# Window attention and convolution on one core: heads in two groups of 64 rows, separate stacks for the transposed pass, maxima sent between partitions

## The chip, the core and the metric
The kernel runs on one core of a Trainium2 chip. The metric is device time in microseconds (us) of one execution; 1663.28 us is the median of three runs before the change.

## The reference, cut to what matters
The input is 2 images of 128 channels, 128 x 128 pixels. Two layers, each with a group normalisation (32 groups) ahead of it and a residual sum behind:
```
x = x + attention(_gn(x))     # L0
x = x + conv3x3(_gn(x))       # L1

g = clip((x*ac_w + ac_b)*x, 0, 6);  qkv = einsum(g, qkv_w)      # 3 x 128 channels
q, k, v: windows of 8x8 pixels (64 tokens), 16 heads of 8 channels
attn = softmax(q @ k.T * 8**-0.5) ; o = attn @ v                # 64 x 64 per window and head
out = einsum(o, proj_w) + proj_b
```
There are 512 windows, and a 64 x 64 score matrix for each of them and each head.

## The kernel before
The kernel goes through each image in 32 units of 8 windows (512 tokens). A unit passes seven stages named by letters, which overlap: `G` (the clipped product, led by 4 iterations), `H` (its f16 high and low halves, 3), `B` (Q, K and V products for unit n + 2), `C` (scores and row maxima for unit n + 1), `D` (first half of the transposed pass for unit n), `E` (its second half, for n - 1), `R` (residual and statistics, n - 2). `iterations` (L189) peels the first and last iterations and runs the middle in a loop whose turn holds `BUFS` = 3 units. Each engine has its own program in a fixed order written by hand in `one`; `after(engine, semaphore, unit)` (L171) is the wait for a step of a unit. After the 32 units of an image come 16 units of the convolution (`conv_one`).

A head has only 8 channels. Q and K are therefore kept in f16 with high and low halves, three parts of 8 rows each (24 rows a head), and four heads share a stack of 96 partitions. TensorE computes the product (`project`, L850), ScalarE copies its high half (L475 for Q, L485 for K), VectorE takes the low half (L681, L688), and SP writes both to a scratch in DRAM (`write`, L261: two DMAs) and reads them back in the stacked order: Q in one DMA (L286), K in four (L290), one for each place of a head in the block diagonal of `k_stack`. TensorE's `scores` (L866) then has 8 matmuls for a pair of windows: 64 tokens of Q times the block-diagonal K of four heads, 256 columns. VectorE takes row maxima (`row_max`, L668). When the four pairs of a unit are through, TensorE transposes the maxima (L976), ScalarE and VectorE make two halves of them (L469, L675), and SP writes them to DRAM (L274) and reads them into rows 96 to 103 of `q_stack` (L277). There they meet the constant rows of `k_stack` (-4096, set by L444 with `mask4`), so that the transposed scores come with the maximum subtracted. `scores_t` (L878) has 32 matmuls of 64 columns a pair, over all 128 rows; ScalarE takes the exponential of 1024 columns (`exps`, L457); `weigh` (L891) multiplies by V in fp32 with 16 matmuls of 18 columns, which the trace shows as 32. Outputs are divided (L657, L660), turned (`turn`, L913), copied in two halves (`turned`, L464) and projected (`output`, L920).

SP has one program and issues all DMAs in its order; a wait on it holds all that stands behind it. In PSUM, bank `GA` (6) takes Q's product and the turned output, bank `GB` (7) K's and V's products and the projected output.

## Time and profile before

| | us |
|---|---|
| median of 3 runs | 1663.28 |
| lowest, highest | 1657.38, 1670.82 |
| the profiled execution | 1678.25 |
| its span | 1676.5 |
| mean granted TensorE clock | 0.828 of full |

The span is the time between the first and the last instruction of the profiled execution. The attention of the first image lies between about 60 and 680 us of it, that of the second between about 890 and 1490 us; the convolutions follow each. A block of matmuls in the timeline shows the time from the start of its first to the end of its last, the tail of the last one in the array included. PEld is the weight load, which overlaps PE. PEclk is the granted clock as a share of 2.4 GHz, 0.50 being 1.2 GHz.

### The profile page before, as it was taken

The numbers are of one execution on the slowest core, as the hardware profiler recorded it, in microseconds if no ns is written. First come the engines' busy times: TensorE is split into PE (matmuls) and PEld (weight loads), VectorE is DVE, ScalarE is ACT, GpSimd is POOL, SyncE is SP. The second block draws the span as 40 slices with busy tenths as digits, with TensorE's granted clock in tenths as the row PEclk, the third lists the DMA queues.
The fourth block names the chain that finished last, engine by engine and source line by source line (L and its number), as shares of the span: only waits on it lengthen the run. The fifth ranks groups of instructions, "written<-read, shape, count | busy, mean of one in ns | idle before, by whom it ended". The sixth has DMA issues, their size and how long they took to land. (4 is left out here: it accounts for less than half of the span.)

```text
span 1676.5 us, 57125 instructions
## 1 busy us (share of the span) xinstructions
PE 1296.1 (77%) x23523; PEld 854.3 (51%) x23523; DVE 1005.9 (60%) x1379; ACT 782.4 (47%) x1107; POOL 380.2 (23%) x245
## 2 busy tenths in 40 slices
PE   1388787887878888597874888888889888859876
PEld 0166565555655666433322656656656666643332
DVE  7555445454544454399994555455654565439998
ACT  3545444444544453344432545454544465435443
POOL 5001111111111110255551111111111111025665
PEclk9778768887887797599995888788985799859998
DMA  5223222232322231012232322332322233200111
GB/s 221 76 91 108 79 75 92 81 90 82 108 83 82 81 115 48 1 55 96 100 130 98 117 85 92 93 95 83 118 83 80 89 113 98 66 2 38 50 50 63
DMA packets 113491, 142.86 MB, mean 85 GB/s; under 512 B 19440, under 2 KB 89584, under 8 KB 112240
## 3 DMA queue, kind: packets, MB, share of 16 engines
q1 hardware_dynamic: 113264, 139.31, 26.1%
q8 instruction: 206, 3.38, 0.8%
q14 instruction: 21, 0.17, 0.0%
HBM read 70.06 MB, written 69.21 MB: 83 GB/s over the span
## 5 line engine op out<-in xcount | busy, mean ns | idle before, releaser
L457 ACT ACTIVATE work<-ps,ws 128x1024 f32<-128x1024 f32 x256 | 285.0, 1113 | 490.4 <-PE ps L886 485.9
L668 DVE TENSOR_REDUCE m_all<-ps 128x16 f32<-128x1024 f32 x256 | 311.9, 1219 | 181.1 <-PE ps L873 179.2
L904 PEld LDWEIGHTS ps<-v_ext,work 128*64 128x64 f32 x8192 | 320.2, 158 | 81.6 <-ACT work L457 64.8
L904 PE MATMUL ps<-v_ext,work 128*64 128x18 f32 x8192 | 328.7, 225 | 39.4 <-ACT work L457 30.2
L873 PE MATMUL ps<-k_stack,q_stack 96*64 96x256 f16 x2048 | 190.3, 315 | 162.7 <-DMA k_stack<-stack_scratch 93.7
L372 POOL TENSOR_TENSOR g_lo<-work,g_hi 128x512 f16<-128x512 f32 x64 | 74.2, 1159 | 1003.0 <-ACT g_hi L493 1003.0
L873 PEld LDWEIGHTS ps<-k_stack,q_stack 96*64 96x64 f16 x2048 | 107.5, 123 | 269.1 <-issue 252.9
L886 PEld LDWEIGHTS ps<-q_stack,k_stack 128*64 128x64 f16 x8192 | 178.4, 124 | 75.6 <-issue 75.3
L886 PE MATMUL ps<-q_stack,k_stack 128*64 128x64 f16 x8192 | 205.2, 209 | 4.6 <-issue 4.2
L836 PE MATMUL ps<-work,c_hi 128*128 128x512 f16 x384 | 152.2, 396 | 68.4 <-DVE work L756 68.3
L681 DVE TENSOR_TENSOR work<-ps,work 128x512 f16<-128x512 f32 x64 | 44.3, 692 | 242.3 <-ACT work L475 242.3
L543 ACT CAST work<-work 128x640 f16<-128x640 f32 x128 | 91.9, 719 | 147.9 <-DVE work L752 106.4
L756 DVE TENSOR_TENSOR work<-work 128x640 f16<-128x640 f32 x128 | 152.3, 1193 | 5.4 <-ACT work L543 5.1
L837 PE MATMUL ps<-work,c_lo 128*128 128x512 f16 x384 | 151.4, 394 | 0.0
L838 PE MATMUL ps<-work,c_hi 128*128 128x512 f16 x384 | 151.0, 393 | 0.0
L398 POOL TENSOR_TENSOR work<-work 128x640 f32<-128x640 f32 x64 | 113.9, 1782 | 49.1 <-DVE work L756 21.5
L920 PE MATMUL ps<-work,pw 128*128 128x512 f32 x128 | 113.3, 981 | 0.9 <-ACT work L464 0.9
L377 POOL TENSOR_TENSOR img<-img,work 128x512 f32 (+1 forms) x64 | 81.3, 1270 | 126.0 <-ACT work L479 126.0
L836 PEld LDWEIGHTS ps<-work,c_hi 128*128 128x128 f16 x384 | 38.5, 100 | 139.6 <-DVE work L756 81.7
L386 POOL TENSOR_TENSOR work<-work,img 128x1024 f32<-128x1024 f32 x30 | 84.6, 2819 | 102.8 <-DVE work L736 102.8
L752 DVE TENSOR_TENSOR work<-work 128x640 f32<-128x640 f32 x64 | 91.8, 1437 | 4.7 <-issue 2.4
L736 DVE SCALAR_TENSOR_TENSOR work<-ps,ws,work 128x512 f32<-128x512 f32 x128 | 92.3, 742 | 0.5 <-ACT work L527 0.2
(125 smaller groups left out, 1660.3 us busy)
## 6 DMA issues: line engine op xcount, KB each, us to landing
stack_scratch<-work SPq DMA_DIRECT2D x128, 256.0 KB, 2.1
q_stack<-stack_scratch SPq DMA_DIRECT2D x64, 384.0 KB, 3.9
k_stack<-stack_scratch SPq DMA_DIRECT2D x256, 96.0 KB
stack_scratch<-work SPq DMA_DIRECT2D x128, 128.0 KB, 2.1
out_dram<-work SPq DMA_DIRECT2D x32, 512.0 KB, 2.7
img<-in_x_dram SPq DMA_DIRECT2D x8, 1024.0 KB, 14.2
img<-in_x_dram SPq DMA_DIRECT2D x16, 512.0 KB, 3.8
max_scratch<-m_pair SPq DMA_DIRECT2D x64, 32.0 KB, 1.8
```

Source lines behind the costliest of these rows:

```text
L398: g.tensor_tensor(plane[2 * k + 1], column(cx, 1), column(cx, c), op).then_inc(odd_planes, 1)
L457: a.activation(probs[:, p % 2, :], ps[:, ST_B:ST_B + 2, :].rearrange("p w t -> p (w t)"), ACT.Exp, scale=ws[:, R_EXP:R_EXP + 1]).then_inc( ...
L668: v.tensor_reduce(m_all[:, 0, :, p, :], ps[:, S_B:S_B + 2, :].rearrange("p h (g j k) -> p (h g) j k", g=2, k=WIN), AX.X, ALU.max).then_inc ...
L736: v.scalar_tensor_tensor(out=outputs(c_out[par], to), in0=ps[:, PLANES * par + m, :], scalar=ws[:, col:col + 1], in1=outputs(c_out[par], old),
L756: v.tensor_tensor(x_lo[:, i, :, :], plane[i], x_hi[:, i, :, :], ALU.subtract).then_inc(x_lo_done, 1)
L836: t_.matmul(o, lhs_hi, rhs_hi, start=first, stop=False)
L837: t_.matmul(o, lhs_lo, rhs_hi, start=False, stop=False)
L838: return t_.matmul(o, lhs_hi, rhs_lo, start=False, stop=last)
L873: mm = t_.matmul(ps[64 * w:64 * w + 64, S_B + h, gg * 256:gg * 256 + 256], q_stack[0:ROWS, mc, 2 * h + gg, tok], k_stack[0:ROWS, mc, 2 * h ...
L886: mm = t_.matmul(ps[64 * e:64 * e + 64, ST_B + w, hp * WIN:(hp + 1) * WIN], k_stack[:, md, g, j + e, tok], q_stack[:, md, g, tok], start=T ...
L904: mm = t_.matmul(ps[64 * w:64 * w + 64, PV_B + p // 2, col:col + VC], probs[:, p % 2, at:at + WIN], v_ext[:, md, 2 * p + w, hp, :], start= ...
L920: t_.matmul(ps[:, GB, :], pw[:, :], o_t, start=True, stop=True).then_inc(proj_done, 1)
```

## The change
The 16 heads are kept in two groups of 64 partitions (`HR` = 2), and each group in four stacks (`HG` = 4) of two heads (`HJ` = 2): 48 rows. A score matmul takes 48 rows, 64 stationary columns and 128 moving columns, and writes one half of the PSUM partitions; row group r writes bank `S_B + r`. So it uses a quarter of the array, and `scores` has 16 of them a pair. The transposed pass no longer uses the same stacks: `scores_t` takes plain K (`k_pl`) as the stationary side and block-diagonal Q (`q_bd`) as the moving side, 50 rows with the two rows of maxima, 128 columns, 16 matmuls a pair. So Q and K are both read from DRAM twice, once for each pass, in the stage before each; each stack has two buffers in place of three. The maxima's halves go in four DMAs from 32 partitions of `m_pair` each straight to one row of `q_bd`. The loop's turn holds 6 units. K's product moves to the head of the iteration, V's product moves to bank `GA` behind Q's, the output takes `GB` after K. ScalarE copies the turned output at once. Constants are set by memsets alone; the projection's input channels are permuted as the weights are loaded, in two DMAs.

```diff
--- before.py
+++ after.py
...
-HG, HJ = 4, 4
+HR, HG, HJ = 2, 4, 2
 PAIRS = UW // 2
 PARTS = 3
 ROWS = HJ * HD * PARTS
-MROWS = 2 * HJ
+HROWS = HD * PARTS
 HP = HEADS // 2
 VC = 2 * HD + 2
 BUFS = 3
+TWO = 2
+TURN = 6
...
-        q_stack = sb("q_stack", [P, BUFS, HG, UT], F16)
-
-
-        k_stack = sb("k_stack", [P, BUFS, HG, HJ, UT], F16)
+        q_pl = sb("q_pl", [P, TWO, HG, UT], F16)
+        k_bd = sb("k_bd", [P, TWO, HG, HJ, UT], F16)
+
+        k_pl = sb("k_pl", [P, TWO, HG, UT], F16)
+        q_bd = sb("q_bd", [P, TWO, HG, HJ, UT], F16)
...
-        m_all = sb("m_all", [P, 2, HG, PAIRS, HJ])
+        m_all = sb("m_all", [P, 2, HEADS, PAIRS])
...
-            first, turns = 2, (UNITS - 6) // BUFS
+            first, turns = 2, (UNITS - 6) // TURN
             for i in range(-4, first):
                 if i == -2 and late:
                     late()
-                one(i, i % BUFS, active(i))
+                one(i, i % TURN, active(i))
+            for i in range(first + turns * TURN, UNITS + 2):
+                one(i, i % TURN, active(i))
...
-            return ps[rows, GB, :].rearrange("p (a d) -> p a d", d=HD)
+            return ps[rows, GA, :].rearrange("p (a d) -> p a d", d=HD)
...
-            sp.wait_ge(pool_set, 12)
-            sp.wait_ge(act_step, 9)
+            sp.wait_ge(pool_set, 10)
 
             for b in range(BATCH):
                 def one(i, m, on):
                     n = i + b * UNITS
-                    n_r = HD * PARTS
-
-                    def write(d, mb, which):
-                        lo, hi, into, sent = ((q_lo_done, q_hi_done, q_in, q_sent),
-                                              (k_lo_done, k_hi_done, k_in, k_sent))[which]
-                        after(sp, into, d - 1)
+                    def write(d, which):
+                        lo, hi, sent = ((q_lo_done, q_hi_done, q_sent), (k_lo_done, k_hi_done, k_sent))[which]
                         after(sp, lo, d)
                         after(sp, hi, d)
-                        to = stackd[mb, which]
+                        to = stackd[(m + 2) % BUFS, which]
                         sp.dma_start(to[:, 0:2, :], qk[:, 2 * which:2 * which + 2, :]).then_inc(sent, 16)
                         sp.dma_start(to[:, 2, :], qk[:, 1 + which, :]).then_inc(sent, 16)
+
+                    def plain(to, src, event):
+                        rows = src.rearrange("(r g a) s t -> r (a s) g t", r=HR, g=HG)
+                        for r in range(HR):
+                            sp.dma_start(to[64 * r:64 * r + ROWS, :, :], rows[r]).then_inc(event, 16)
+
+                    def spread(to, src, event):
+                        rows = src.rearrange("(r g j d) s t -> r j (d s) g t", r=HR, g=HG, j=HJ)
+                        for r in range(HR):
+                            for j in range(HJ):
+                                at = 64 * r + HROWS * j
+                                sp.dma_start(to[at:at + HROWS, :, j, :], rows[r, j]).then_inc(event, 16)
                     if "D" in on:
-                        after(sp, m_in, n - 1)
                         after(sp, m_hi_done, n)
                         after(sp, m_lo_done, n)
-                        sp.dma_start(maxd[m], m_pair[:, :, :]).then_inc(m_sent, 16)
-                        after(sp, m_sent, n)
-                        after(sp, st_done, n - BUFS)
-                        sp.dma_start(q_stack[ROWS:ROWS + MROWS, m, :, :].rearrange("r g (p t) -> r (g p) t", p=PAIRS),
-                                     maxd[m].rearrange("(a j) s t -> (j s) a t", j=HJ)).then_inc(m_in, 16)
+                        after(sp, st_done, n - TWO)
+                        for r in range(HR):
+                            for k in range(2):
+                                at = 64 * r + ROWS + k
+                                sp.dma_start(q_bd[at:at + 1, m % TWO, :, :, :].rearrange("o g j (p t) -> o (g j p) t", p=PAIRS),
+                                             m_pair[32 * r:32 * r + 32, k, :]).then_inc(m_in, 16)
                     if "B" in on:
-                        d, mb = n + 2, (m + 2) % BUFS
-                        k_rows = stackd[mb, 1].rearrange("(g j d) s t -> j (d s) g t", g=HG, j=HJ)
-                        write(d, mb, 0)
-                        write(d, mb, 1)
-                        after(sp, q_sent, d)
-                        after(sp, st_done, d - BUFS)
-                        sp.dma_start(q_stack[0:ROWS, mb, :, :],
-                                     stackd[mb, 0].rearrange("(g r) s t -> (r s) g t", g=HG)).then_inc(q_in, 16)
-                        after(sp, k_sent, d)
-                        for j in range(HJ):
-                            sp.dma_start(k_stack[n_r * j:n_r * j + n_r, mb, :, j, :], k_rows[j]).then_inc(k_in, 16)
+                        after(sp, qd_in, n)
+                        after(sp, kd_in, n)
+                        write(n + 2, 1)
+                        write(n + 2, 0)
+                        after(sp, kc_in, n + 1)
+                        after(sp, qc_in, n + 1)
+                        after(sp, k_sent, n + 2)
+                        after(sp, s_done, n)
+                        spread(k_bd[:, m % TWO, :, :, :], stackd[(m + 2) % BUFS, 1], kc_in)
+                        after(sp, q_sent, n + 2)
+                        plain(q_pl[:, m % TWO, :, :], stackd[(m + 2) % BUFS, 0], qc_in)
+                    if "C" in on:
+                        if "B" not in on:
+                            after(sp, qd_in, n)
+                            after(sp, kd_in, n)
+                        after(sp, st_done, n + 1 - TWO)
+                        spread(q_bd[:, (m + 1) % TWO, :, :, :], stackd[(m + 1) % BUFS, 0], qd_in)
+                        plain(k_pl[:, (m + 1) % TWO, :, :], stackd[(m + 1) % BUFS, 1], kd_in)
...
-                    def turned(d, h):
-
-                        after(act, ot_done, d, h + 1)
+                    def turned(d):
+
+                        after(act, ot_done, d)
                         after(act, proj_done, d - 1)
-                        a.copy(o_t[:, 256 * h:256 * h + 256], ps[:, GA, 256 * h:256 * h + 256]).then_inc(ot_out, 1)
+                        a.copy(o_t, ps[:, GA, :]).then_inc(ot_out, 1)
 
                     if "D" in on:
                         after(act, mt_done, n)
-                        after(act, m_sent, n - 1)
+                        after(act, m_in, n - 1)
                         a.mul(m_pair[:, 0, :], ps[0:PAIRS * HEADS, M_B, 0:P], 1.0 / PAIR_MAX).then_inc(m_hi_done, 1)
+                    if "B" in on:
+                        after(act, k_done, n + 2)
+                        after(act, k_sent, n + 1)
+                        a.copy(qk[:, 2, :], ps[:, GB, :]).then_inc(k_hi_done, 1)
...
-                        v.tensor_reduce(m_all[:, 0, :, p, :],
-                                        ps[:, S_B:S_B + 2, :].rearrange("p h (g j k) -> p (h g) j k", g=2, k=WIN), AX.X,
+                        v.tensor_reduce(m_all[:, 0, :, p],
+                                        ps[:, S_B:S_B + 2, :].rearrange("p r (a k) -> p (r a) k", k=WIN), AX.X,
                                         ALU.max).then_inc(max_done, 1)
                     if peeled(i, 0) and b:
                         after(dve, out_done, b * CUNITS - 1)
@@ -677,16 +680,15 @@
                     if "C" in on:
                         row_max(0)
                     if "B" in on:
+                        after(dve, k_hi_done, n + 2)
+                        v.tensor_tensor(qk[:, 3, :], ps[:, GB, :], qk[:, 2, :], ALU.subtract).then_inc(k_lo_done, 1)
...
-                        for h in range(2):
-                            for gg in range(2):
-                                for w in range(2):
-                                    tok = slice((2 * p + w) * WIN, (2 * p + w + 1) * WIN)
-                                    mm = t_.matmul(ps[64 * w:64 * w + 64, S_B + h, gg * 256:gg * 256 + 256],
-                                                   q_stack[0:ROWS, mc, 2 * h + gg, tok],
-                                                   k_stack[0:ROWS, mc, 2 * h + gg, :, tok], start=True, stop=True)
+                        settle(pe)
+                        for g in range(HG):
+                            for w in range(2):
+                                tok = slice((2 * p + w) * WIN, (2 * p + w + 1) * WIN)
+                                for r in range(HR):
+                                    rows = slice(64 * r, 64 * r + ROWS)
+                                    mm = t_.matmul(ps[64 * w:64 * w + 64, S_B + r, g * P:g * P + P],
+                                                   q_pl[rows, (m + 1) % TWO, g, tok], k_bd[rows, (m + 1) % TWO, g, :, tok],
+                                                   start=True, stop=True)
                         mm.then_inc(s_done, 1)
 
                     def scores_t(d, md, p):
 
                         after(pe, exp_done, d, p)
+                        settle(pe)
                         for w in range(2):
                             tok = slice((2 * p + w) * WIN, (2 * p + w + 1) * WIN)
-                            for hp in range(HP):
-                                g, j = hp // 2, 2 * (hp % 2)
-                                for e in range(2):
-                                    mm = t_.matmul(ps[64 * e:64 * e + 64, ST_B + w, hp * WIN:(hp + 1) * WIN],
-                                                   k_stack[:, md, g, j + e, tok], q_stack[:, md, g, tok],
+                            for g in range(HG):
+                                h, c = g // 2, g % 2
+                                for r in range(HR):
+                                    rows = slice(64 * r, 64 * r + ROWS + 2)
+                                    at = w * 256 + h * P
+                                    mm = t_.matmul(ps[64 * c:64 * c + 64, ST_B + r, at:at + P],
+                                                   k_pl[rows, md % TWO, g, tok], q_bd[rows, md % TWO, g, :, tok],
...
+                        project(1, GB, k_done)
                     if "C" in on:
-                        after(pe, q_in, n + 1)
-                        after(pe, k_in, n + 1)
+                        after(pe, qc_in, n + 1)
+                        after(pe, kc_in, n + 1)
                         scores(0)
                     if "E" in on:
                         weigh(n - 1, me, 1)
+                        scores_t(n - 1, me, 2)
                     if "B" in on:
-                        after(pe, g_lo_done, n + 2)
-                        after(pe, q_lo_done, n + 1)
+                        after(pe, v_out, n + 1)
                         after(pe, ot_out, n - 2)
-                        if peeled(i, -2) and b:
-                            after(pe, m3_out, b * CUNITS - 1)
                         project(0, GA, q_done)
-                    if "E" in on:
-                        scores_t(n - 1, me, 2)
-                    if "R" in on:
-                        if "C" in on:
-                            after(pe, v_out, n + 1)
-                        output(n - 2)
                     if "C" in on:
                         scores(1)
                     if "E" in on:
                         weigh(n - 1, me, 2)
-                    if "B" in on:
-                        after(pe, v_out, n + 1)
-                        after(pe, res_done, n - 2)
-                        project(1, GB, k_done)
+                    if "R" in on:
+                        if "B" in on:
+                            after(pe, k_lo_done, n + 2)
+                        after(pe, res_done, n - 3)
+                        output(n - 2)
                     if "E" in on:
                         scores_t(n - 1, me, 3)
-                        if "B" in on:
-                            after(pe, q_lo_done, n + 2)
-                        after(pe, ot_out, n - 2)
-                        turn(n - 1, 0)
+                    if "B" in on:
+                        after(pe, q_lo_done, n + 2)
+                        v_rows()
                     if "C" in on:
                         scores(2)
                     if "E" in on:
                         weigh(n - 1, me, 3)
                     if "D" in on:
                         after(pe, m_in, n)
+                        after(pe, qd_in, n)
+                        after(pe, kd_in, n)
                         scores_t(n, m, 0)
-                    if "B" in on:
-                        after(pe, k_lo_done, n + 2)
-                        v_rows()
+                    if "E" in on:
+                        if "B" in on:
+                            after(pe, v_out, n + 2)
+                        after(pe, ot_out, n - 2)
+                        turn(n - 1, 0)
...
```

SP's program, one unit in the peeled iterations behind the loop, before (`max_scratch` and `stack_scratch` are DRAM, `m_pair` holds the maxima, `work` the halves of Q and K):
```order
L274 DMA max_scratch<-m_pair 64x256
L277 DMA q_stack<-max_scratch 8x16x128
L268 DMA stack_scratch<-work 128x1024
L269 DMA stack_scratch<-work 128x512
L268 DMA stack_scratch<-work 128x1024
L269 DMA stack_scratch<-work 128x512
L286 DMA q_stack<-stack_scratch 96x4x512
L290 DMA k_stack<-stack_scratch 24x4x512 x4
```
and now:
```order
L288 DMA q_bd<-m_pair 1x32x128 x4
L267 DMA stack_scratch<-work 128x1024
L268 DMA stack_scratch<-work 128x512
L267 DMA stack_scratch<-work 128x1024
L268 DMA stack_scratch<-work 128x512
L280 DMA k_bd<-stack_scratch 24x4x512 x4
L273 DMA q_pl<-stack_scratch 48x4x512 x2
L280 DMA q_bd<-stack_scratch 24x4x512 x4
L273 DMA k_pl<-stack_scratch 48x4x512 x2
```
The eleven issues of a unit are twenty. K's write comes first, K's read for the scores stands behind both writes, and the second reading (`q_bd`, `k_pl`) is of the unit one ahead of its use.

TensorE's program in the loop, from the transpose of the maxima on, before (`k_stack,q_stack` are scores at L873, `q_stack,k_stack` transposed scores, L904 weighted sums, L836 to L838 first Q's product, then K's):
```order
L976 MATMUL ps<-ident,m_all 128x128
L873 MATMUL ps<-k_stack,q_stack 64x256 x8
L904 MATMUL ps<-v_ext,work 64x18 x16
L836 MATMUL ps<-g_hi,w_hi 128x512
L837 MATMUL ps<-g_hi,w_lo 128x512
L838 MATMUL ps<-g_lo,w_hi 128x512
L886 MATMUL ps<-q_stack,k_stack 64x64 x32
L920 MATMUL ps<-work,pw 128x512
L873 MATMUL ps<-k_stack,q_stack 64x256 x8
L904 MATMUL ps<-v_ext,work 64x18 x16
L836 MATMUL ps<-g_hi,w_hi 128x512
L837 MATMUL ps<-g_hi,w_lo 128x512
```
and now (L876 scores, L892 transposed scores, L910 weighted sums, L838 to L840 first K's product, then Q's):
```order
L986 MATMUL ps<-ident,m_all 128x128
L838 MATMUL ps<-g_hi,w_hi 128x512
L839 MATMUL ps<-g_hi,w_lo 128x512
L840 MATMUL ps<-g_lo,w_hi 128x512
L876 MATMUL ps<-k_bd,q_pl 64x128 x16
L910 MATMUL ps<-v_ext,work 64x18 x16
L892 MATMUL ps<-q_bd,k_pl 64x128 x16
L838 MATMUL ps<-g_hi,w_hi 128x512
L839 MATMUL ps<-g_hi,w_lo 128x512
L840 MATMUL ps<-g_lo,w_hi 128x512
L876 MATMUL ps<-k_bd,q_pl 64x128 x16
L910 MATMUL ps<-v_ext,work 64x18 x16
```
K's product has come ahead of the first scores, and Q's stands behind the first transposed block.

## Rows read from the trace of the kernel before

**Rows 1.** The page's engine totals: busy us (share of the span) xinstructions
```profile
PE 1296.1 (77%) x23523; PEld 854.3 (51%) x23523; DVE 1005.9 (60%) x1379; ACT 782.4 (47%) x1107; POOL 380.2 (23%) x245
```

**Rows 2.** Timeline of SP's queue, first and last issue of the maxima in each batch (columns: start us, us, engine line op out<-in xcount)
```profile
82.21 0.52 SPq L274 DMA_DIRECT2D max_scratch<-m_pair  x1
...
645.26 0.45 SPq L274 DMA_DIRECT2D max_scratch<-m_pair  x1
...
914.62 0.49 SPq L274 DMA_DIRECT2D max_scratch<-m_pair  x1
...
1464.76 0.45 SPq L274 DMA_DIRECT2D max_scratch<-m_pair  x1
```

**Rows 3.** Timeline of all engines, 302 to 320 us: one passage of K through DRAM
```profile
302.05 0.68 DVE L688 TENSOR_TENSOR work<-ps,work 128x512 f16<-128x512 f32 x1
...
303.27 0.93 SPq L269 DMA_DIRECT2D stack_scratch<-work  x1
...
305.68 1.56 SPq L290 DMA_DIRECT2D k_stack<-stack_scratch  x4
...
310.60 0.63 PE L873 MATMUL ps<-k_stack,q_stack 96*64 96x256 f16 x8 [1.86 <-DMA k_stack<-stack_scratch]
...
318.26 0.58 ACT L485 CAST work<-ps 128x512 f16<-128x512 f32 x1 [1.28 <-PE ps L838]
...
318.87 0.69 DVE L688 TENSOR_TENSOR work<-ps,work 128x512 f16<-128x512 f32 x1
```

**Rows 4.** Waits of all engines (us in total, times, longest us), and two timeline rows of PE
```profile
PE ps L873 <- DMA k_stack<-stack_scratch: 93.7, 45, 3.7
...
PE ps L873 <- issue: 67.9, 18, 6.3
...
402.69 0.33 PE L976 MATMUL ps<-ident,m_all 128*128 128x128 f32 x1 [0.25 <-DVE m_all L668]
406.87 1.06 PE L873 MATMUL ps<-k_stack,q_stack 96*64 96x256 f16 x8 [3.85 <-issue]
```

**Rows 5.** Windows: us, busy of PE, PEld, DVE, ACT, POOL, then PEclk, DMA share, GB/s
```profile
310.00:311.00 1.00, 0.40 (x8) 0.41 (x10) 0.00 (x0) 0.00 (x0) 0.00 (x0) 1.00 0.00 0
312.00:313.00 1.00, 1.00 (x8) 0.44 (x7) 0.49 (x1) 0.00 (x0) 0.00 (x0) 0.50 0.14 35
980.00:1460.00 480.00, 408.11 (x9300) 298.26 (x9302) 252.45 (x367) 241.61 (x366) 62.23 (x52) 0.83 0.31 92
```

**Rows 6.** Timeline, 300 to 303.2 us: TensorE's blocks with the clock at 1.00
```profile
300.41 0.39 PE L836 MATMUL ps<-g_hi,w_hi 128*128 128x512 f16 x1
...
300.85 0.38 PE L838 MATMUL ps<-g_lo,w_hi 128*128 128x512 f16 x1
...
301.16 0.70 PE L886 MATMUL ps<-q_stack,k_stack 128*64 128x64 f16 x32
...
301.78 0.44 PE L913 MATMUL ps<-ident,work 128*128 128x128 f32 x2
...
302.19 0.63 PE L873 MATMUL ps<-k_stack,q_stack 96*64 96x256 f16 x8
...
303.14 1.11 PE L904 MATMUL ps<-v_ext,work 128*64 128x18 f32 x32 [0.32 <-ACT work L457]
```

**Rows 7.** The page's costliest groups (columns as on the page: busy, mean ns | idle before)
```profile
L457 ACT ACTIVATE work<-ps,ws 128x1024 f32<-128x1024 f32 x256 | 285.0, 1113 | 490.4 <-PE ps L886 485.9
L668 DVE TENSOR_REDUCE m_all<-ps 128x16 f32<-128x1024 f32 x256 | 311.9, 1219 | 181.1 <-PE ps L873 179.2
```

**Rows 8.** The page's DMA issues: KB each, median us from issue to landing
```profile
q_stack<-stack_scratch SPq DMA_DIRECT2D x64, 384.0 KB, 3.9
k_stack<-stack_scratch SPq DMA_DIRECT2D x256, 96.0 KB
stack_scratch<-work SPq DMA_DIRECT2D x128, 128.0 KB, 2.1
```

117 lines of the change are left out of this document (51 added, 66 removed).

## The prediction
> **What bounds the kernel now.** The profiled execution took 1678.25 us (span 1676.5), 0.9% over the median of the three timed runs, 1663.28. The engine totals come first: TensorE is the busiest, 77% of the span [rows 1]. To see where the time lies I took the issue of the maxima (L274), once per unit, as a beat: 31 periods from 82.21 to 645.26 us and 31 from 914.62 to 1464.76 us [rows 2], together 1113.2 us for 62 periods, **17.95 us per unit**. The other 563 us (start, convolutions, pipeline ends) the change hardly touches.
>
> In the timeline one unit shows a ring [rows 3]. K's low half leaves VectorE at 302.05 + 0.68; its write is issued until 304.2; the four reads that wait for it start at 305.68; TensorE, idle for 1.86 us, starts the next unit's scores at 310.60 when they have landed. The same queue of TensorE has that iteration's K product only shortly before 318.26, where ScalarE, idle for 1.28 us, copies it; K's low half comes at 318.87. From one low half to the next it is 16.8 us: 0.7 for itself, 7.9 of write and read, 7.7 inside TensorE's queue from scores to K product, 0.6 of copy. So **the ring through DRAM** ends last in many units, with TensorE's own work close behind.
>
> Two rows tell of what the ring costs besides. TensorE stood before the first scores for 93.7 us on DMAs, and for 67.9 us in 18 stops without a releaser, the longest 6.3 us, a typical one 3.85 us at 406.87 us [rows 4]. Two of the 18 belong to the fillings of the two batches; 16 are as many as the loop of three units has turns (2 x 8). I read those, (67.9 - 2 x 6.3) / 16 = 3.5 us each, as the price of a back jump, which here lies over the wait for DMAs. And the granted clock is 1.00 before such a gap, 0.50 at 312 us after TensorE has resumed (the 1.2 GHz level), and over 480 us of the second batch 0.83 [rows 5]: a third of the time at half speed.
>
> **The change part by part**, per unit, at the 2.4 GHz level.
> *Scores and transposed scores.* Eight 256-column matmuls take 0.63 us, of which about 0.2 is the tail of the last one; 32 of 64 columns take 0.70 us and hold the engine 0.50 us, 16 ns each [rows 6]. So column halves already run side by side (64 columns at 2.4 GHz are 27 ns). Afterwards both kinds are 16 matmuls of 128 columns on quarters of the array. Bounds for a block: all four quarters together 16 x 53 / 4 = 0.21 us; only column halves together 0.43 us; one after another 0.85 us. No row shows 64-row matmuls. I take 0.25 us (16 times the 16 ns pace [rows 6]), nearest in form. Saved: 4 x (0.45 - 0.25) + 4 x (0.50 - 0.25) = 1.8 us.
> *Changes of array shape.* From L838 to L886 the distance is 0.31 us against (300.85 - 300.41) / 2 = 0.22 us between products, so a switch costs 0.09 us; L886 to L913 is 0.62 us against 0.50 us, again 0.1 [rows 6]. Before, 10 switches per unit; afterwards 17, since weighted sums (full rows) and scores (half rows) alternate. +0.7 us. The upper bound is a whole tail of 0.2 us at each of the 17: 3.4 in place of 1.0, so +2.4 us, and the block gain would be gone; I take the rows' own 0.1. The Trainium skill (TensorEngine Tiling (Array Packing), Key Properties) says that a change of tiling mode, not of tile alone, drains TensorE. By that rule, the trace agrees in kind and puts it at half a tail; a full drain is in rival 3.
> *TensorE's sum.* At the fast level, a unit before is scores 1.8, transposed scores 2.0, weighted sums 4 x 0.9, two products 1.3, V 0.8, output 1.0, transposes 1.2, switches 1.0: about 12.7 us ([rows 6]; V is 48 times 16 ns, the output four times a product's 0.22 us and a little more). After: 12.7 - 1.8 + 0.7 = **11.6 us**.
> *The order.* K's product goes to the head of the iteration, V behind Q. The ring is now the one of Q. Walk, t = 0 at the first scores: row maximum until 1.7 (1.22 each [rows 7]), K's low half until 2.4, its write at once; weighted sums until 1.2, transposed block, exponentials until 3.0 (1.11 each [rows 7]), Q copy until 3.6, low half until 4.3, write issued until 5.2 (Q's product ends at 2.5). Then the four K reads are issued (4 x 0.39 [rows 3]), Q's write has landed (2.1 us after issue [rows 8]) at 7.0, two Q reads until 7.8, and 3.4 us after the last issue (as 307.2 to 310.6 [rows 3]) all has landed: the ring is **11.2 us** instead of 16.8.
> *Rest of the walk.* TensorE: second weighted sums from 3.0, output 4.0 to 4.9, transposed block, V until 6.1, scores, weighted sums at 7.1 (exponentials end 7.0, held by the residual's evacuation), transposed block 8.3; ScalarE then evacuates V and g and ends the next exponentials at 9.9; weighted sums until 10.9, transposed block, transposes, K product at 12.9. TensorE idles 0.6 + 0.8 us in it. So **13.0 us** with all at full clock; ScalarE and VectorE were busy 241.61 and 252.45 us in some 27 units [rows 5], 8.9 and 9.4 us each: neither binds.
> *DMA queue.* 11 issues per unit become 20 (4 one-row sends of maxima, 4 writes, 12 reads): 20 x 0.39 = 7.8 us of SP. The second reading of the stacks (6 issues, 2.3 us) comes after Q's reads, at 7.8 to 10.2, lands by 13.6 to 15, and the next K write waits for it at 13.0 + 2.4 = 15.4: hidden, by less than 2 us. If that cover is gone, it is added to the ring. Bytes: 1.6 MB become 2.34 MB (two more stacks of 384 KB [rows 8]). At 92 GB/s for a share of 0.31 [rows 5] a MB costs 3.4 us of all engines: 7.9 us of a unit, 60%.
> *Maxima.* They go straight to one partition, without the round through DRAM. That round is not on the ring (issued at the unit's end, wanted in its second half): zero either way. Merged o_t copy: 0.15 us of ScalarE, covered by TensorE. The new waits of the output on K's low half and of V on Q's are met at 2.4 and 4.3, before 4.0 and 5.3: zero.
> *Clock.* Gaps of 0.6 and 0.8 us stand in place of one of 2 to 4 us; the products behind 300.41 us have lengths of the full level (0.38 us) with gaps of 0.3 us about them [rows 6]. I leave 0.6 us per unit: 13.6 us.
> *Back jumps.* Six units per turn: 2 x 4 = 8 in place of 16, but now uncovered: 3.5 us each and some 2.5 us lost to half speed behind it (5 us at 0.50) = 48 us. Bounds: 4 us each (32 us) to 8 us each (64 us).
> *Start.* Memsets and mask rows change, and the projection weights arrive in 32-byte pieces; bounds -4 to +6 us, as ScalarE's and VectorE's start-up work overlaps the image load. Zero.
>
> **Sum.** 62 x 13.6 = 843, plus 48 = 891 in place of 1113: -222 us. 1678 - 222 = 1456 us for a profiled execution; the shown median lies 15 us under its own, so **1441 us**. Its own range: 12.8 per unit with 32 us of jumps (-287) to 14.4 with 64 (-156): 1376 to 1507.
>
> **Rivals.**
> 1. *The ring stays in the lead.* 60% of DMA share with the second reading in the way of K's write: ring and second reading in line cost 4.5 us more than 11.2, so 15.7 per unit, with the jumps hidden in it again: 62 x 15.7 = 973, -140: 1523 us. For it: the slack is under 2 us. Against: K's and Q's reads are ahead of the second reading in the queue.
> 2. *The clock keeps falling.* With 0.83 as before, 13.0 / 0.83 = 15.7 us, jumps 8 x 3.5 = 28 us: 62 x 15.7 + 28 = 1001, -112: 1551 us. For it: the gaps at 310 and 403 us were followed by half speed [rows 4, 5]. Against: no such gap is left outside jumps.
> 3. *No packing over row halves.* 0.43 us per block: 8 x 0.18 = 1.4 us more, x 62 = +89: 1530 us. With switches at a whole tail besides, 1.7 us more, +105: 1635 us, hardly a change. The page named above, read at its strictest, speaks for that far end.
> 4. *Slower.* Quarter blocks run one after another, their weight loads and shape changes between them. The decisive point: with jumps spread over the units the forecast is 14.4 us, so the period is back at 17.95 when a block holds TensorE for (17.95 - 14.4) / 8 + 0.25 = 0.69 us. At 0.85 us (16 x 53 ns in a row) it is 14.4 + 4.8 = 19.2 us: 62 x 19.2 = 1190, +77: 1740 us. For it: no row shows this form. Against: 32 narrow loads and matmuls passed in 0.50 us [rows 6], 16 ns where a single file would take 27.
> 5. *It doesn't shorten anything*, since a wait I don't see (a late residual, second buffers of two in place of three) holds the period: 1650 to 1670.
>
> **Chances.** Forecast 0.60; rival 1 0.12; rival 2 0.08; rival 3 0.08 (a quarter of it near no change); rival 4 0.07; rival 5 0.05; together 1.00. A measurement of this kernel tells 1% from no change. Faster 0.60 + 0.12 + 0.08 + 0.06 = 0.86, within 1% 0.02 + 0.05 = 0.07, slower 0.07. The range takes the forecast's own and rivals 1 to 3 but for their far ends: **1375 to 1580**.
>
> **What will show it.** In the changed trace: the beat of the maxima near 13.6 us; new score blocks starting 16 ns apart and lasting about 0.45 us with the tail; the first scores waiting for no DMA outside jumps; K's low half 2.4 us behind the first scores; a granted clock above 0.93 in the attention stages; 8 stops of about 3.5 us before the K product, now the first instruction of a turn. A block over 0.69 us would make rival 4 true; scores waiting for q_pl, or K's write waiting for q_bd, rival 1; a clock still at 0.83 with no DMA wait, rival 2.

## The result: slower, with TensorE at half clock

The changed kernel takes **1818.29 us** (median of four runs, 1816.38 to 1822.06); the kernel before took 1664.78 beside it. The ratio is **1.093**, 95% interval 1.088 to 1.098. The forecast was 1441 us, in a range of 1375 to 1580: wrong in size and in sign. The profiled execution took 1822.06 us, span 1820.3, at a mean granted clock of 0.670; the other three had 0.640 to 0.642. Below, one of the two runs each of experiments nine and eleven fell in a slower state of the chip (1670.86 and 1720.25 us), so their times are those of the other run.

The page of the changed kernel, the lines that answer to [rows 1, 7, 8] (columns as on that page; the PEclk line holds the granted clock in tenths, 40 slices):
```profile
PE 1474.0 (81%) x21475; PEld 930.1 (51%) x21475; DVE 991.4 (54%) x1379; ACT 772.1 (42%) x1039; POOL 376.5 (21%) x243
...
PEclk9996656555555655599975555565555565558999
...
q1 hardware_dynamic: 168960, 187.58, 38.8%
...
L671 DVE TENSOR_REDUCE m_all<-ps 128x16 f32<-128x1024 f32 x256 | 312.2, 1220 | 371.8 <-PE ps L876 371.8
L910 PE MATMUL ps<-v_ext,work 128*64 128x18 f32 x8192 | 446.9, 262 | 60.2 <-ACT work L462 60.1
L462 ACT ACTIVATE work<-ps,ws 128x1024 f32<-128x1024 f32 x256 | 284.4, 1111 | 303.7 <-PE ps L892 302.2
...
L876 PE MATMUL ps<-k_bd,q_pl 48*64 48x128 f16 x4096 | 151.3, 289 | 18.4 <-DMA q_pl<-stack_scratch 11.1
...
q_pl<-stack_scratch SPq DMA_DIRECT2D x128, 192.0 KB, 3.7
```
VectorE and ScalarE work as long as before (1220 and 1111 ns) and wait longer, both for TensorE's score blocks. The wait of the scores for DMAs is nearly gone: 11.1 us against 93.7 [rows 4]. The PEclk line shows nines only at its ends and between the two batches; the attention stages read mostly 5 and 6 tenths. The nines up to 142 us are an error of the record, since the blocks there have the lengths that they have at 0.50:
```profile
105.00:120.00 15.00, 14.74 (x221) 9.96 (x223) 6.83 (x10) 6.21 (x10) 0.30 (x1) 1.00 0.36 94
...
110.34 1.90 PE L910 MATMUL ps<-v_ext,work 128*64 128x18 f32 x32
```
So this execution's 0.670 is too high, and the 0.64 of the other three is nearer.

Windows of the changed kernel (columns as in [rows 5]), the attention stages and two short stretches:
```profile
80.00:720.00 640.00, 560.98 (x9599) 384.94 (x9599) 285.23 (x417) 280.70 (x385) 69.12 (x58) 0.61 0.46 116
980.00:1600.00 620.00, 544.21 (x9452) 371.89 (x9447) 280.18 (x413) 276.94 (x381) 68.66 (x58) 0.58 0.48 119
390.00:421.00 31.00, 29.30 (x444) 19.43 (x446) 14.16 (x21) 11.82 (x17) 2.38 (x2) 0.50 0.41 106
423.00:426.00 3.00, 1.91 (x66) 1.51 (x54) 1.91 (x3) 1.60 (x3) 0.00 (x0) 1.00 0.95 218
```
TensorE is busy 88% of the stages, more than before (408.11 of 480, 85%), and the clock is 0.61 and 0.58 (the first is 0.56 from 160 us on, without the stretch of the error) where it was 0.83 [rows 5]. From 390 to 421 us it is busy 29.30 of 31 us and stands at 0.50, the 1.2 GHz level, throughout. No stop of TensorE explains that: the 1.7 us in which it idles are spread over the stretch.

Its timeline, the same blocks at both levels (405 to 409 us at 0.50, 423 to 425 us at 1.00), and the maxima in SP's queue, which answer to [rows 2]:
```profile
405.78 0.64 PE L876 MATMUL ps<-k_bd,q_pl 48*64 48x128 f16 x16
406.87 1.90 PE L910 MATMUL ps<-v_ext,work 128*64 128x18 f32 x32 [0.45 <-ACT work L462]
408.70 0.64 PE L892 MATMUL ps<-q_bd,k_pl 50*64 50x128 f16 x16
...
422.79 0.42 PE L876 MATMUL ps<-k_bd,q_pl 48*64 48x128 f16 x16
423.13 1.11 PE L910 MATMUL ps<-v_ext,work 128*64 128x18 f32 x32
424.18 0.42 PE L892 MATMUL ps<-q_bd,k_pl 50*64 50x128 f16 x16
```
```profile
76.17 1.26 SPq L288 DMA_DIRECT2D q_bd<-m_pair  x2
...
411.75 2.41 SPq L288 DMA_DIRECT2D q_bd<-m_pair  x4
432.26 3.11 SPq L288 DMA_DIRECT2D q_bd<-m_pair  x4
...
721.28 1.14 SPq L288 DMA_DIRECT2D q_bd<-m_pair  x2
...
972.07 1.16 SPq L288 DMA_DIRECT2D q_bd<-m_pair  x2
...
1605.34 1.14 SPq L288 DMA_DIRECT2D q_bd<-m_pair  x2
```
The beat is (721.28 - 76.17 + 1605.34 - 972.07) / 62 = **20.62 us** instead of 17.95, which is 1278.4 us in place of 1113.2 for the 62 periods: +165.2 us. All else became 21 us shorter (the beat's first row comes 6 us earlier, the way between the batches is 18.6 us shorter, the end 3 us longer). The sum, +144, is the measured difference of the two profiled executions. At the full level the block fits the prediction: from 422.79 to the weighted sums' start it is 0.34 us, where 0.25 and a switch of 0.1 were forecast (the rows show only their sum). It is hardly ever at that level.

The waits of the changed kernel (engine, line waited for: us, times, longest):
```profile
DVE m_all L671 <- PE ps L876: 371.8, 138, 6.2
ACT work L462 <- PE ps L892: 302.2, 134, 5.5
...
DVE st L698 <- POOL img L387: 212.4, 56, 5.1
...
PE ps L838 <- issue: 20.5, 6, 3.8
```
The third line is a second surprise: VectorE stands 212.4 us, in 56 of 64 units, before the statistics of the image (L698) for GpSimd's residual addition. The kernel before has the same wait in as many places, but shorter:
```profile
DVE st L696 <- POOL img L377: 78.3, 56, 4.9
```
The last line of the changed kernel's waits has the stops at the back jumps, six and not eight: a loop of four turns jumps back three times, in two batches.

### The profile page after: what moved, and what is told of

It reads as the page before. It is cut to its first block and busy times, and to the rows that moved or that the text cites. A ratio compares the mean times of both kernels' runs of the same rounds, so it can differ in the third digit from the quotient of the medians.

```text
span 1820.3 us, 53510 instructions
## 1 busy us (share of the span) xinstructions
PE 1474.0 (81%) x21475; PEld 930.1 (51%) x21475; DVE 991.4 (54%) x1379; ACT 772.1 (42%) x1039; POOL 376.5 (21%) x243
## 5 line engine op out<-in xcount | busy, mean ns | idle before, releaser
L671 DVE TENSOR_REDUCE m_all<-ps 128x16 f32<-128x1024 f32 x256 | 312.2, 1220 | 371.8 <-PE ps L876 371.8
L910 PE MATMUL ps<-v_ext,work 128*64 128x18 f32 x8192 | 446.9, 262 | 60.2 <-ACT work L462 60.1
L910 PEld LDWEIGHTS ps<-v_ext,work 128*64 128x64 f32 x8192 | 419.1, 207 | 108.9 <-ACT work L462 72.2
L462 ACT ACTIVATE work<-ps,ws 128x1024 f32<-128x1024 f32 x256 | 284.4, 1111 | 303.7 <-PE ps L892 302.2
L838 PE MATMUL ps<-work,c_hi 128*128 128x512 f16 x384 | 151.2, 394 | 68.3 <-DVE work L758 68.2
L876 PE MATMUL ps<-k_bd,q_pl 48*64 48x128 f16 x4096 | 151.3, 289 | 18.4 <-DMA q_pl<-stack_scratch 11.1
L876 PEld LDWEIGHTS ps<-k_bd,q_pl 48*64 48x64 f16 x4096 | 94.5, 144 | 136.9 <-issue 133.5
L698 DVE BATCH_NORM_STATS2 st<-img (+1 forms) x64 | 44.4, 693 | 212.4 <-POOL img L387 212.4
L892 PE MATMUL ps<-q_bd,k_pl 50*64 50x128 f16 x4096 | 153.1, 292 | 0.0
L488 ACT ACTIVATE work<-ps,vecs,ws 128x512 f32<-128x512 f32 x64 | 49.7, 777 | 243.2 <-PE ps L926 243.2
L840 PE MATMUL ps<-work,c_hi 128*128 128x512 f16 x384 | 150.5, 392 | 0.0
L892 PEld LDWEIGHTS ps<-q_bd,k_pl 50*64 50x64 f16 x4096 | 95.4, 145 | 101.1 <-issue 93.6
L500 ACT COPY v_ext<-ps 64x512 f32<-64x512 f32 x128 | 75.9, 593 | 118.8 <-PE ps L910 103.3
L919 PE MATMUL ps<-ident,work 128*128 128x128 f32 x256 | 76.0, 392 | 61.5 <-ACT v_ext L500 60.9
L838 PE MATMUL ps<-g_hi,w_hi 128*128 128x512 f16 x128 | 79.1, 618 | 44.6 <-issue 20.5
L838 PEld LDWEIGHTS ps<-work,c_hi 128*128 128x128 f16 x384 | 38.3, 100 | 139.7 <-DVE work L758 82.1
```

The costliest lines, as they stand in the source:

```text
L462: a.activation(probs[:, p % 2, :], ps[:, ST_B:ST_B + 2, :].rearrange("p w t -> p (w t)"), ACT.Exp, scale=ws[:, R_EXP:R_EXP + 1]).then_inc( ...
L671: v.tensor_reduce(m_all[:, 0, :, p], ps[:, S_B:S_B + 2, :].rearrange("p r (a k) -> p (r a) k", k=WIN), AX.X, ALU.max).then_inc(max_done, 1)
L838: t_.matmul(o, lhs_hi, rhs_hi, start=first, stop=False)
L840: return t_.matmul(o, lhs_hi, rhs_lo, start=False, stop=last)
L876: mm = t_.matmul(ps[64 * w:64 * w + 64, S_B + r, g * P:g * P + P], q_pl[rows, (m + 1) % TWO, g, tok], k_bd[rows, (m + 1) % TWO, g, :, tok] ...
L892: mm = t_.matmul(ps[64 * c:64 * c + 64, ST_B + r, at:at + P], k_pl[rows, md % TWO, g, tok], q_bd[rows, md % TWO, g, :, tok], start=True, s ...
```

## The experiments

Two questions: what took the clock, and where the ring's gain went. As to the first, one theory is that the granted clock follows **how much of the array is at work**, and that the new forms (48 or 50 rows of a tile in place of 96 or 128, half the multiplies or less) took it. Its rivals are the new order, the added DMA traffic, and the added changes of array shape. A ratio is always to the kernel before, timed on the same chip (1676 to 1685 us there, against 1664.78 beside the changed kernel itself); a clock is the mean of the profiled execution (nine's is that of its one run), and between runs of one kernel it differs by up to 0.04. In four and thirteen the record errs at the start as it does in the changed kernel; their clocks are too high by 0.01 to 0.03, an estimate from the lengths of the weighted sums.

**One: double the work** of the changed kernel. Every quarter matmul of both kinds is issued twice, to the same place.
```diff
-                                    mm = t_.matmul(ps[64 * w:64 * w + 64, S_B + r, g * P:g * P + P],
-                                                   ...
+                                    for again in range(2):
+                                        mm = t_.matmul(ps[64 * w:64 * w + 64, S_B + r, g * P:g * P + P],
+                                                       ...
```


> The changed kernel with every quarter-array score matmul (scores and transposed scores) issued twice; the second overwrites the first with the same values. A block then streams 32 x 128 columns on quarters, as long as the kernel before streamed in a block (0.43 us at full clock, 0.85 at half). Theory A (the full clock is granted only where TensorE's time is filled with streaming columns; the change halved the streaming of the scores): the mean granted clock rises from 0.67 to over 0.80 and the time falls under 1818, to 1550 to 1700 us, although there is more work. Theory B (quarter-array matmuls don't count for the clock): clock 0.60 to 0.67, 8 x 0.43 us more a unit at half clock, 1990 to 2050 us. Theory C (the new order with its many short stops costs the clock, not the matmuls' form): as B.

Measured: 1756.05 us, ratio 1.040 (1.027 to 1.054), clock 0.742. Twice the matmuls in the blocks, and less time: 1756 against 1818 us, ratio 1.040 against 1.093. The gain is smaller than theory A asked (under 1700 us, a clock over 0.80), but no account in which TensorE's work or its switches bind at a fixed clock allows that.

**Two: the same matmuls on all 128 rows.** The other half's rows of the 16 matmuls meet data that don't belong to them, so the scores of the two groups of heads are added to each other. Here and in ten, thirteen and sixteen the rows of `q_pl` that hold no data are set to zero once, at the start.
```diff
-                                    rows = slice(64 * r, 64 * r + ROWS)
+                                    rows = slice(0, P)
...
-                                    rows = slice(64 * r, 64 * r + ROWS + 2)
+                                    rows = slice(0, P)
```


> The changed kernel with each score matmul over all 128 rows (both groups of heads at once) in place of 48 or 50; columns, counts, banks and order as in the changed kernel. The scores of the two groups are added to each other, so the output is not the reference's. A block streams 16 x 128 columns on halves of the array: 0.43 us at full clock, twice the quarter blocks. Theory A: like the doubled kernel, clock over 0.80, 1550 to 1700 us. Theory B: also over 0.80. Theory C: clock 0.60 to 0.67 and 1990 to 2050 us.

Measured: 1680.09 us, ratio 1.004 (1.000 to 1.008), clock 0.828. The number of matmuls and columns, the order and the DMAs are those of the changed kernel; the packing of row halves is lost; and it is 1680 us in place of 1818 (1.004 against 1.093). DMA traffic (133 GB/s at 80 to 600 us here) is excluded as what takes the clock.

**Three and five: the two parts of the change apart.** Three keeps the stacks, forms and maxima of before, and takes the new order on all engines with six units per turn. Five is the reverse: new forms, stacks, direct maxima and six per turn, in the old order.
```diff
+TURN = 6
...
-                        write(d, mb, 0)
                         write(d, mb, 1)
-                        after(sp, q_sent, d)
+                        write(d, mb, 0)
+                        after(sp, k_sent, d)
...
```


> The kernel before with the new order alone: K's product at the head, V behind Q, K's write first, the output behind K, the turned output copied at once, six units a turn; stacks, score matmuls (96 and 128 rows, half arrays) and the maxima's way through DRAM as before. Theories A and B: TensorE streams as much as before without the long wait for K's reads, so the mean granted clock is over 0.90, the period 14 to 15 us and the time 1470 to 1550 us. Theory C: clock under 0.70 and 1850 us or more.

> The changed kernel with the order of the kernel before on TensorE, ScalarE, VectorE and in SP's writes and reads (Q first, V in bank GB, the turned output in two copies): the quarter-array scores, separate stacks, direct maxima and six units a turn remain. Theory B2 (the clock goes by what the matmuls put on the array, and quarter blocks put less on it, in any order): granted clock 0.62 to 0.72 and 1780 to 1900 us, the slowness of the change is in the form. Theory C2 (form and new order together): clock over 0.78, 1640 to 1720 us.

Measured: three 1695.11 us, 1.010 (1.005 to 1.015), clock 0.819; five 1787.39 us, 1.061 (1.054 to 1.068), clock 0.657. So the **forms** bring the low clock and most of the loss in either order; the order does not. (Five has the stacks and the direct maxima too, but so has two, with a clock of 0.828.) But the order alone, which takes the ring away and takes 14 back jumps down to 6, brings nothing either: both theories A and B had expected a clock over 0.90 and 1470 to 1550 us of it. That is the second question, and the timeline of experiment three answers it, here 403 to 411 us:
```profile
403.06 0.68 PE L884 MATMUL ps<-q_stack,k_stack 128*64 128x64 f16 x32
...
403.32 1.21 ACT L496 COPY v_ext<-ps 64x512 f32<-64x512 f32 x2 [1.27 <-PE ps L902]
...
404.56 0.62 ACT L503 CAST g_hi<-work 128x512 f16<-128x512 f32 x1
...
405.25 1.15 POOL L373 TENSOR_TENSOR g_lo<-work,g_hi 128x512 f16<-128x512 f32 x1 [14.93 <-ACT g_hi L503]
...
406.37 1.26 POOL L378 TENSOR_TENSOR img<-img,work 128x512 f32 x1
...
407.96 0.69 DVE L694 BATCH_NORM_STATS2 st<-img  x1 [3.88 <-POOL img L378]
...
408.57 1.21 DVE L667 TENSOR_REDUCE m_all<-ps 128x16 f32<-128x1024 f32 x1
...
409.84 0.33 PE L975 MATMUL ps<-ident,m_all 128*128 128x128 f32 x1 [1.47 <-DVE m_all L667]
...
410.04 0.38 PE L834 MATMUL ps<-g_hi,w_hi 128*128 128x512 f16 x1
...
410.77 0.63 PE L871 MATMUL ps<-k_stack,q_stack 96*64 96x256 f16 x8
```
The idle times behind the rows lead through four engines' work in single file: the weighted sums let ScalarE copy V, then cast g; GpSimd forms g's low half (14.93 us idle, waiting for it), and only behind that, in program order, adds the residual; VectorE's statistics wait 3.88 us for it, and the last row maximum is queued behind them; its transpose, the K product and the next scores come last. This chain replaced the ring. The wait in it is VectorE's, 3.88 us here and 211.5 us in all, against 78.3 in the kernel before.

**Four and six: fill the array from outside.** One, then two, full-array matmuls of 512 columns ahead of each score block of the changed kernel, overwritten by it.
```diff
+                        for pad in range(1):
+                            t_.matmul(ps[:, S_B, :], w_hi[:, 0, :], c_hi[:, 0:4, :].rearrange("p a d -> p (a d)"), start=True, stop=True)
```


> The changed kernel with one full-array matmul of 512 columns on constant weights ahead of each score block (4 a unit); its result is overwritten by the scores. Pure extra work: 4 x 0.43 us a unit at half clock, 4 x 0.22 at full. Theory A: mean clock over 0.75, time 1500 to 1700 us. Theory B: the full-array columns count, so the same, if less. Theory C: clock 0.60 to 0.67, 62 x 1.7 us more, 1900 to 1950 us.

> The changed kernel with two full-array matmuls of 512 columns ahead of each score block (8 a unit): as much extra streaming as doubling (e1) or widening (e2) gave, 8 x 0.43 us at half clock, but on 128 rows and 128 columns and in one piece. Theory A (only streaming time counts): clock 0.74 to 0.83 as in e1 and e2, 1700 to 1800 us. Theory B2 (what counts is how full the array is over the stretches in which scores and weighted sums alternate; extra work in one place doesn't help the other stretches): clock 0.68 to 0.72, 1880 to 1930 us.

Measured: one 1864.44 us, 1.106 (1.095 to 1.116), clock 0.686; two 1771.33 us, 1.053 (1.047 to 1.060), clock 0.727. The first filler cost more than it gave, the second gave back more than both cost. Neither expectation for six (under 1800 us at a clock of 0.74 or more; 1880 us or more at 0.72 or less) fits both of its numbers, so this pair doesn't decide between them.

**Seven and eight: GpSimd's two steps exchanged,** the residual ahead of g's low half, in experiment three (seven) and in the changed kernel (eight).
```diff
-                    if "H" in on:
-                        after(pool, g_hi_done, n + 3)
-                        g.tensor_tensor(g_lo[:, m, :], g32, g_hi[:, m, :], ALU.subtract).then_inc(g_lo_done, 1)
                     if "R" in on:
...
+                    if "H" in on:
+                        after(pool, g_hi_done, n + 3)
+                        g.tensor_tensor(g_lo[:, m, :], g32, g_hi[:, m, :], ALU.subtract).then_inc(g_lo_done, 1)
```


> The kernel of e3 (old forms, new order) with two instructions of GpSimd exchanged: the residual sum goes ahead of g's low half. In e3 the chain weighted sums, V's copy, g's high half, g's low half, residual sum, statistics, last row maximum, transpose of the maxima (403.2 to 409.8 us) sets the period at full clock, not the DMA ring. If so, the last row maximum comes 1.5 to 2.5 us earlier, the period at full clock falls from 16 to 17 us to 14.5 to 15, the clock rises over 0.85 and the time falls to 1560 to 1620 us, under the kernel before. If the chain isn't the bound: 1680 to 1700 us.

> The changed kernel with the same exchange on GpSimd. VectorE no longer stands 3.9 us for the residual ahead of the last row maximum. If the half clock is the bound (TensorE busy 88% of the attention stages at a clock near 0.6), the gain is small: 1770 to 1815 us, clock 0.65 to 0.70. If the stops of TensorE are what lowers its clock, the clock rises over 0.75 and the time falls under 1700 us.

Measured: seven **1534.45 us**, 0.912 (0.906 to 0.919), clock 0.868; eight 1800.45 us, 1.072 (1.066 to 1.077), clock 0.633. On the old forms, behind the new order, the exchange is worth 0.098 of 1680, 164 us, more than the 75 to 135 us that were expected; on the new ones, where half-clock TensorE binds, about a fifth of that. The exchange in the old order was not tried. Waits and windows of seven:
```profile
POOL img L375 <- ACT work L484: 715.2, 64, 18.5
POOL g_lo L378 <- ACT g_hi L503: 276.9, 64, 33.9
```
```profile
80.00:600.00 520.00, 446.05 (x11028) 333.91 (x11028) 294.84 (x434) 287.97 (x400) 72.64 (x60) 0.88 0.32 99
850.00:1300.00 450.00, 394.07 (x9503) 295.24 (x9504) 258.14 (x379) 253.14 (x355) 65.29 (x54) 0.86 0.33 102
```
GpSimd now waits mainly for the residual's own source, and the wait of the statistics, 212.4 us in the changed kernel, is 10.2 us in two places in seven (211.5 in three).

**Nine: take work away** from seven. In the looped units the score matmuls stream 128 of their 256 columns.
```diff
-                                    mm = t_.matmul(ps[64 * w:64 * w + 64, S_B + h, gg * 256:gg * 256 + 256],
+                                    js = HJ if isinstance(i, int) else HJ // 2
+                                    mm = t_.matmul(ps[64 * w:64 * w + 64, S_B + h, gg * 256:gg * 256 + 64 * js],
...
```


> The kernel of e7 in which, in the looped 24 units of each image, each score matmul (not the transposed ones) takes 128 of its 256 columns; the maxima of the other heads are stale, so the output is not the reference's. Form (half array, 96 rows) unchanged, 4 x 512 array-columns of streaming less a unit; nothing is added. Theory A (the streaming share decides the clock): the clock falls from 0.87 to 0.70 to 0.80 and the time rises from 1534 to 1600 to 1720 us although TensorE has less to do. Theory B (the quarter form decides): clock 0.85 to 0.90 and 1480 to 1530 us.

Measured: 1643.20 us (one run), clock 0.78. That is 109 us **slower** than seven, with less to compute and the same order, DMAs and shapes. Its windows, from the longer, profiled run (clock 0.757):
```profile
80.00:600.00 520.00, 450.49 (x9956) 341.27 (x9957) 276.05 (x401) 267.40 (x370) 67.70 (x56) 0.73 0.31 95
980.00:1400.00 420.00, 371.82 (x7455) 283.23 (x7454) 203.72 (x299) 201.73 (x278) 50.90 (x42) 0.64 0.28 85
```
TensorE is busy 450.49 us where seven has 446.05: the columns saved came back as slower ones, in every matmul of the stage, and fewer units passed in the window (VectorE 276.05 us of work against 294.84).

**Ten, eleven, thirteen, sixteen: a ladder of array work** on the changed kernel with the exchange. Ten: all 128 rows (as two). Eleven: matmuls doubled (as one). Thirteen: all 64 rows of each quarter, the added ones giving zeros. Sixteen: both of the last.
```diff
-                                    rows = slice(64 * r, 64 * r + ROWS)
+                                    rows = slice(64 * r, 64 * r + 64)
...
-                                    rows = slice(64 * r, 64 * r + ROWS + 2)
+                                    rows = slice(64 * r, 64 * r + 64)
```


> The widened kernel of e2 (all 128 rows in each score matmul, outputs not the reference's) with GpSimd's exchange of e7. Streaming and form as in e7 (half arrays) but with separate stacks and direct maxima. Both theories: clock 0.84 to 0.90, 1500 to 1560 us. If separate stacks, their DMAs or the direct maxima cost something by themselves it is seen here: over 1600 us.

> The doubled kernel of e1 (each quarter-array matmul twice) with GpSimd's exchange. The same array-columns of streaming as e10, in quarter form with 17 changes of shape. Theory A: clock and time near e10, over 0.82 and under 1600 us. Theory B: clock 0.70 to 0.76 and 1690 to 1750 us.

> The changed kernel with GpSimd's exchange (e8) and all 64 rows of each quarter in every score matmul, the added rows of zeros (and of the constant against zeros), so the output is unchanged. Same columns, same shape, same times. If the clock goes by the rows that an instruction names: clock from 0.63 to over 0.68 and under 1770 us. If rows count nothing: 0.61 to 0.66 and 1780 to 1820 us.

> The doubled kernel of e11 with all 64 rows of each quarter in every score matmul (the added rows are zeros, the output is unchanged). Quarter form, 17 changes of shape, but the same cells times columns as the half blocks of e10. If cells times streaming decide the clock: from 0.773 to 0.84 to 0.88, and 1550 to 1610 us. If something of the quarter form remains: clock 0.77 to 0.82, 1640 to 1710 us.

Measured, ordered by the multiplies of a unit's eight blocks (rows times columns of the tile, times columns streamed, times matmuls):

| experiment | millions | us | ratio | clock |
|---|---|---|---|---|
| eight (changed, exchange) | 8 x 6.4 = 51 | 1800.45 | 1.072 | 0.633 |
| thirteen (64 rows) | 8 x 8.4 = 67 | 1763.31 | 1.051 (1.045 to 1.057) | 0.696, too high |
| nine (old forms, half of the score columns) | 4 x 6.3 + 4 x 16.8 = 92 | 1643.20, one run | none | 0.78 |
| eleven (doubled) | 103 | 1685.84, one run | none | 0.773 |
| seven (old forms) | 4 x 12.6 + 4 x 16.8 = 117 | 1534.45 | 0.912 | 0.868 |
| sixteen (doubled, 64 rows) | 134 | 1644.40 | 0.976 (0.969 to 0.984) | 0.863 |
| ten (128 rows) | 134 | 1566.54 | 0.936 (0.930 to 0.942) | 0.872 |

One window of each, 80 to 600 us: eight, thirteen, sixteen, ten.
```profile
80.00:600.00 520.00, 460.69 (x8042) 321.62 (x8035) 245.55 (x354) 238.41 (x329) 60.52 (x50) 0.57 0.49 122
```
```profile
80.00:600.00 520.00, 453.66 (x8173) 317.66 (x8173) 251.75 (x362) 241.54 (x334) 60.41 (x50) 0.67 0.50 124
```
```profile
80.00:600.00 520.00, 442.45 (x12844) 330.64 (x12848) 275.32 (x402) 267.23 (x374) 67.87 (x56) 0.87 0.54 138
```
```profile
80.00:600.00 520.00, 431.51 (x9798) 330.64 (x9798) 291.85 (x425) 282.20 (x392) 71.63 (x59) 0.88 0.59 144
```
The clock follows the order of the ladder to within 0.01 (nine's 92 holds for the looped units, the others have 117). Eleven fell between its two expectations; sixteen has the clock of the one and the time of the other. Eight and thirteen differ, but for the zeros set at the start, in nothing but products with zeros; and the time goes down by 2%. Thirteen's 0.67 is too high: until 156 us its record reads 1.00 beside weighted sums of 1.90 us, the length at 0.50. From 160 to 600 us the clock goes from 0.56 in eight to 0.61 in thirteen, from 980 to 1600 us from 0.55 to 0.59: a small step, but the intervals of the ratios lie apart. Along the four windows busy time falls (460.69 to 431.51) while the clock rises (0.57 to 0.88): what counts is how much of the array works and for how many columns, not how long something runs. Sixteen has ten's clock but not its time: its 128 more matmuls and loads per unit show as 37 us of stops without a releaser ahead of the blocks and the weighted sums, against 7 us in ten, and it keeps 17 changes of shape where ten has 10. That these two make up the 78 us was not tried. Nor was it separated whether a row counts in the matmul or in its weight load: two, ten and thirteen widen both, and only nine cuts the columns and leaves the loads alone.

**Fourteen: shape changes alone.** Ten with four quarter matmuls of 8 columns ahead of each score block: eight more changes of shape per unit, next to no work.
```diff
+                        for w in range(2):
+                            for r in range(HR):
+                                t_.matmul(ps[64 * w:64 * w + 64, S_B + r, 0:8], q_pl[64 * r:64 * r + ROWS, (m + 1) % TWO, 0, 0:64],
+                                          k_bd[64 * r:64 * r + ROWS, (m + 1) % TWO, 0, 0, 0:8], start=True, stop=True)
```


> The kernel of e10 (half-array form, 128 rows; output not the reference's) with four quarter-array matmuls of 8 columns at the head of each of the four score blocks of a unit; they are overwritten. That adds 8 changes of array shape a unit and next to no streaming. If the changes of shape are what separates e11 (0.773, 1703 us) from e10 (0.872, 1567 us): clock 0.75 to 0.81 and 1650 to 1720 us. If it is the form of the streaming itself: clock 0.84 to 0.87 and 1575 to 1620 us (8 x 0.1 to 0.2 us x 62 = 50 to 100 us at the most).

Measured: 1558.36 us, 0.929 (0.922 to 0.935), clock 0.872. They take neither clock nor time from ten (1566.54 us, 0.872); at 0.1 us each I would have priced them at 50 us. So the changes of shape are excluded as what takes the clock, where TensorE's work is that of ten.

**Twelve and fifteen: the loop's turns.** Seven with 3 and with 24 units per turn.
```diff
-TURN = 6
+TURN = 24
```


> The kernel of e7 with three units a turn of the loop in place of six: 16 back jumps in place of 8. By the prediction's term each costs 3.5 us of stop and 2.5 us of lost clock: +48 us, 1560 to 1610 us. If a back jump is hidden behind other waits: under 1550 us.

> The kernel of e7 with 24 units a turn, so that the loop has one turn per image and no units are taken twice: 2 loops of one turn in place of 8 back jumps. By the difference of e12 to e7, (1609 - 1534) / 8 = 9.4 us a jump, it is 6 to 8 x 9.4 us faster: 1460 to 1480 us. By the prediction's 6 us: 1485 to 1500 us. If longer straight code makes the engines wait for instructions: 1530 us or more.

Measured: twelve 1609.48 us, 0.960 (0.955 to 0.964), clock 0.835; fifteen **1465.27 us**, 0.872 (0.868 to 0.876), clock 0.906, the fastest of all, over six runs. Back jumps are 14, 6 and 0: eight of them cost (0.960 - 0.912) x 1680 = 80 us, six (0.912 - 0.872) x 1680 = 67 us, **10 to 11 us each**, give or take 2 by the intervals. The maxima of seven in SP's queue show one, behind two steps of 14.25 us:
```profile
374.15 0.45 SPq L275 DMA_DIRECT2D max_scratch<-m_pair  x1
388.39 0.45 SPq L275 DMA_DIRECT2D max_scratch<-m_pair  x1
402.65 0.46 SPq L275 DMA_DIRECT2D max_scratch<-m_pair  x1
423.53 0.45 SPq L275 DMA_DIRECT2D max_scratch<-m_pair  x1
```
The next step is 20.9 us, 6.6 more: TensorE stands 3.31 us before the K product at 404.15, and the granted clock is 0.50 from 404 to 410 us behind that stop. The step behind it is 15.65 us, 1.4 more; the rest was not traced. Page and windows of fifteen:
```profile
PE 1166.6 (79%) x23523; PEld 778.6 (53%) x23523; DVE 1000.6 (68%) x1379; ACT 784.0 (53%) x1043; POOL 382.1 (26%) x245
...
PEclk9869999999899995999976699989999999779998
```
```profile
80.00:600.00 520.00, 444.75 (x11096) 329.90 (x11097) 315.69 (x470) 301.90 (x418) 86.46 (x69) 0.91 0.32 98
850.00:1300.00 450.00, 381.22 (x9884) 287.35 (x9885) 270.07 (x411) 266.18 (x369) 72.15 (x59) 0.92 0.33 100
```
TensorE has 307 us less busy time than in the changed kernel (1474.0), for a form that issues more matmuls and twice the multiplies.

## Why the prediction was wrong

**Clock: the step that failed.** "I leave 0.6 us per unit: 13.6 us." It read the clock of 0.83 as the mark of gaps, saw that the gaps would go, and let the clock recover. The gaps went and the clock fell to 0.6. At that level TensorE is busy 0.88 x 20.62 = 18.1 us of a unit, where 11.6 was forecast for the full level, and so it binds. Experiments two, nine and thirteen show the cause: the step took half the multiplies away and priced the saved columns alone, not what all the other matmuls of the stage pay when the clock goes. The Trainium skill (TensorE: Matmul & The Clock Gate, Part 1: The HAM clock gate) says that the gate is set by how busy TensorE has been. If busy means that something runs, this trace disagrees: 29.30 of 31 us busy at 0.50. The measurement decides; a busy share in the profile doesn't tell whether the clock will be granted.

**Nor would the clock alone have been enough.** The miss is 1818 - 1441 = 377 us. Two, with the clock back at 0.828, takes 1680 us, 138 less; ten, with GpSimd's exchange too, 1567 us, 114 less again. So a second step failed, hidden behind the first: the rest of the walk, below. The last 126 us, in which ten's unpacked rows and the back jumps lie, were not taken apart.

**Rival 2** had the right place and the wrong cause and level. It kept 0.83 for gaps that remain (1551 us); nothing in it could go under 0.83, and no case of mine reached 1818 us. **Rival 4**, the one on the slower side, asked for blocks of 0.69 us at full clock; they take 0.34 us with the switch. Its neighbour, the same block at half clock beside everything else at half clock, was the one to write down.

**Blocks and switches: right where the clock is full.** 0.25 us and 0.1 us were forecast, and together they fit the 0.34 us seen where the clock is full. At half clock the block is 0.64 us with its tail, as long as a score block of before at full clock (0.63 [rows 6]): for this block the clock took back what the packing won. A full tail of 0.2 us at the switch, as in rival 3, would leave 0.14 us for the block, under the lower bound of 0.21, so it doesn't show. Fourteen adds that eight more switches don't lengthen a kernel in which TensorE has slack.

**The ring: right, and worth nothing by itself.** Its wait is nearly gone (93.7 to 11.1 us). But the **rest of the walk**, 13.0 us, the second step that failed, left out the chain from V's copy over g, GpSimd and the residual to the statistics and the last row maximum. It follows from the order in which GpSimd issues two steps, and it holds experiment three at its 1.01. A trace of the kernel before shows it already, as 78.3 us that VectorE waits before the statistics, covered there by the ring. With the exchange the undisturbed step is 14.25 us (seven and fifteen, on the old forms; of the new ones, eight's shortest step inside a batch, at a mixed clock, is 16.1 us). Against that 13.0 was 1.2 us short even without the chain.

**Back jumps: stop right, price wrong.** Stops of at most 3.8 us (3.5 forecast), and 6 of them, not 8 (before, 14 and not 16). In all a jump costs 10 to 11 us, not 6, on the old forms near full clock; if that holds for the changed kernel, which no run shows, it is about 63 us where 48 stood. I had counted 2.5 us for half speed behind a stop. The Trainium skill (Runtime: NRT & Kernel Launch, Instruction fetch mechanics) says that a taken branch to a target outside the fetched pages stalls the engine until they are read again; six such stops of 3.4 us on average here, 14 of 3.0 in twelve and none in fifteen, which has no back jump, fit that, though no run here shows the fetch itself.

**Maxima, DMA queue, start: right as far as tested.** The scores wait for DMAs 11.1 us in all with SP's 20 issues per unit and the direct sends in its queue, so these don't bind at 20.62 us a unit. At the pace of the forecast the slack is smaller, as the prediction said: in ten the scores wait 30.5 us for the reads of Q, in 18 places. Outside the beat the kernel gained 21 us where zero was set, most of it between the batches; why was not looked into.

That 1465 us of fifteen lies close to the forecast of 1441 proves nothing for it: fifteen lacks the change's forms and has two edits that the change has not.

## What to carry to other kernels

On one core TensorE's granted clock is a price of the whole stage, and it can fall when a matmul is made narrower or shorter: before shrinking the rows or columns of a small part, ask what share of the array's work it is, and compare at the clock, not only at the matmul (ten with wasted rows beats eight without by 234 us). When a wait is removed, walk every engine's queue in program order for the chain that comes next: here the new order brought nothing until two GpSimd instructions were exchanged, and 164 us with it. Unroll a loop until its back jumps are few; here each cost some 0.7 of an undisturbed step.

## What the runs showed of the hardware

- The record of the granted clock can be wrong at the start of an execution: in three of these (the changed kernel, four, thirteen) it reads 1.00 up to 130 us and more where the weighted sums take the 1.90 us of 0.50, not 1.11.
- TensorE busy 29.30 of 31 us with the clock at 0.50 throughout, on 48 and 50 rows, 64 columns, and with full-array projections between.
- Rows that add only zeros to the result count: from 48 and 50 rows to 64 the clock goes from 0.56 to 0.61 at 160 to 600 us and from 0.55 to 0.59 at 980 to 1600 us; with 128 rows, not all of zeros, it is 0.88 at 80 to 600 us.
- Sixteen matmuls of 128 columns on the four quarters of the array take 0.34 us at full clock up to the start of the next kind, about 0.25 without the switch, which is an estimate of 16 ns each; with the tail they take 0.42 us at full and 0.64 us at half clock.
- Full-array fillers (8 x 512 columns per unit, 118 million multiplies with the blocks) give 0.727, less than about as many in the blocks themselves (117 million, 0.819 in experiment three). Where in the unit the work lies seems to matter too; that is open.
- Removing half of the columns of half of the blocks made a kernel 109 us slower (1643.20 against 1534.45 us).
